# Four-layer graph network on one core: the one-hots of the matrix items read from a padded index row in three pieces

## The chip, the cores and the metric

The kernel runs on one core of one Trainium2 chip. The metric is the device time of one execution in microseconds (us), lower is better, given as the median of several executions. Engines are named as in the profile: PE (TensorE, matrix products), DVE (VectorE), ACT (ScalarE), POOL (GpSimd, which here issues the gathers), SP (SyncE, which here issues most plain transfers). DMA means a transfer between the chip's main memory and the on-chip memory.

## The reference

The input is `x` (6250 nodes x 128 features, float32) and a list of 100,000 edges `src`, `dst`. Four layers follow, each on `relu(layernorm(x))`, each added to `x`:

```
L0: h = f @ Wn.T;  new_h = [h[src], |h[dst]-h[src]|] @ We.T;  s = (h + segment_sum(new_h)) / count;  [f, s] @ Wl.T
L1: two graph transformer layers: scores q[dst].k[src] over 8 heads, clip, exp, segment sums, projection, FFN with GELU
L2: relu(D^-1/2 segment_sum((D^-1/2 f)[src] -> dst) @ W + b)
L3: two GCN convolutions and sigmoid(z @ Wd + bd)
```

Layers L2 and L3 need only sums over edges with weights that the nodes fix. The kernel therefore makes the adjacency matrix once (how many edges go from node i to node j) and does these layers as dense products. For layers L0 and L1 each edge's rows must be gathered.

## The kernel before

Nodes lie in 49 tiles of 128 (`NT`). The edges are sorted and cut into 832 steps of 128 edges (`STEPS`). Three **edge passes**, `diff` (layer L0), `att0` and `att1` (layer L1), go over all 832 steps in 208 groups of four steps (`S4`), four groups to a loop turn; between them lie dense stages, and after them the adjacency products ("the convolutions").

In an edge pass each engine has an order written out by hand (`body`), held together by semaphores. For a group:

- POOL gathers four blocks of 128 rows with four indirect DMAs (L720). The buffers hold several groups, so POOL runs ahead until it waits for a group to be used up (L1795 in the attention passes, the edge sums on PE in `diff`).
- DVE builds the edge one-hot (L1724), subtracts or multiplies gathered and expanded rows (L1771 in `diff`, L1780 in `att`), reduces to scores (L1783), clips (L1786), makes the messages (L1795) and adds PE's edge sums into `ACC` (L1737, L1739, L1742: `sums`).
- PE transposes one-hots (L886), expands rows (L896), sums edges (L914, L916, L918).
- ACT copies transposed one-hots (L1229) and takes `abs` (L1261) or `exp` (L1258).

**Matrix items** build the adjacency matrix beside this. An item is a set of up to 128 edges that share a source tile and a 512-wide group of destinations. For each item DVE writes two 16-bit one-hots by comparing an index row with a number for each edge: `OHS1` (128 wide, L1749) and `OHD` (512 wide, L1750). PE multiplies them (L926) into a bank of 128 x 512 sums, ACT keeps or clears the bank (L1242) and copies it out (L1247), SP stores it. There are 1456 items: 520 in `diff`, 520 in `att0` (in both, 3, 2, 3, 2 for the four groups of a turn) and 416 in `att1` (two for each group). The one-hots go round a ring of five (four in `att1`).

On DVE, the items of the next group are made at these places. In `diff`: after all four `sums` of the body, ahead of the next L1771. In the attention passes: the first item after `sums(1)` and ahead of L1795, which waits for ACT's `exp`; the second (and third) after `sums(2, 3)`, ahead of the next L1780. A body begins by loading four tile numbers into registers (L445).

`IOTA512` is the index row: the numbers 0 to 511 in float16, written once at L1603. L1749 reads its first 128 numbers.

Of the kernel before, what the change touches and what calls it, by code (L numbers as in the profile page):

```python
# [13 lines left out]
F16 = mybir.dt.float16  # L14
U16 = mybir.dt.uint16
I32 = mybir.dt.int32
ALU = mybir.AluOpType
# [3 lines left out]
P = 128  # L21
# [23 lines left out]
LOW = 10  # L45
T4 = 4
W4 = T4 * P
NW = -(-NT // T4)
ITEMS = STEPS + NT * (NW - 1)
CLASSES = NT * NW  # L50
PLAN = {"diff": (0, (3, 2, 3, 2), 5), "att0": (10 * STEPS // PB, (3, 2, 3, 2), 5), "att1": (20 * STEPS // PB, (2, 2, 2, 2), 4)}
SLOTS = 28 * STEPS // PB
SPARE = NW * P * NT
QJ = 7
# [3 lines left out]
NSC = STEPS // SCH  # L58
assert SLOTS >= ITEMS and STEPS // PB == GROUPS // 4 and NQ * QJ == NT and NSC * SCH == STEPS and NW == 13 and W4 == 512
AW = 2 * D + 1  # L60
# [15 lines left out]
def wait(eng, s, what, value, slot=None):  # L76

    if isinstance(value, int) and value <= 0:
        return
    eng.wait_ge(s[what] if slot is None else s[what][slot], value + s.base[what])  # L80
# [25 lines left out]
def build(nc, a, out, debug=None):  # L106
    with ExitStack() as ctx:
        def sb(name, shape, dt=F32):
            return ctx.enter_context(nc.sbuf_tensor(name, shape, dt))

        def sem(name):
            return ctx.enter_context(nc.semaphore(name))
# [5 lines left out]
        placed = [nc.dram_tensor(f"placed{o}", (2 * P * STEPS, 1), I32, kind="Internal").ap() for o in range(2)]  # L118
        adj_all = nc.dram_tensor("adj", ((NW + 2) * P, NT * W4), F32, kind="Internal").ap()
        adj = adj_all.rearrange("(g p) (j w) -> g p j w", p=P, w=W4)  # L120
        adj_blocks = adj_all.rearrange("r (j w) -> (r j) w", w=W4)

# [7 lines left out]
        TILE = [sb(f"TILE{o}", [P, STEPS], I32) for o in range(2)]  # L130
        IDX = [sb(f"IDX{o}", [P, STEPS], I32) for o in range(2)]
        SCR = sb("SCR", [P, 7296])
        ITEM = sb("ITEM", [P, 2 * W4 + 5 * (W4 + P) // 2])
        IOTA512 = sb("IOTA512", [P, W4], F16)
        IOTA = sb("IOTA", [P, P])
        IDENT = sb("IDENT", [P, P])
        ONES = sb("ONES", [P, P])
# [56 lines left out]
        LOK, DREL, KEEP = (Xf[:, i * SLOTS:(i + 1) * SLOTS] for i in range(3))  # L194
        at = 3 * SLOTS
        assert at + 3 * W4 <= NT * D
        STG = [Xf[:, at + i * W4:at + (i + 1) * W4] for i in range(3)] + [ITEM[:, i * W4:(i + 1) * W4] for i in range(2)]
        KEPT = STG[2]
        XS = [Xf[:, at:at + TG * D].rearrange("p (t d) -> p t d", t=TG), ITEM[:, 0:TG * D].rearrange("p (t d) -> p t d", t=TG)]
        assert TG * D <= 2 * W4  # L200
        OHD = ITEM[:, 2 * W4:2 * W4 + 5 * W4 // 2].bitcast(F16).rearrange("p (r w) -> p r w", r=5)
        OHS1 = ITEM[:, 2 * W4 + 5 * W4 // 2:].bitcast(F16).rearrange("p (r w) -> p r w", r=5)
        STORE = {"diff": TILE[0][32:33, :], "att0": TILE[1][32:33, :], "att1": TILE[0][64:65, :]}
        XA = Q
        IOTAK, REACHED = ACC[:, 0:ITEMS], ACC[:, ITEMS:2 * ITEMS]
# [49 lines left out]
        CLASS_SUM = [banks[1], banks[7]]  # L255
# [81 lines left out]
        def kind_of(n):  # L337
            return "att" if n.startswith("att") else "diff"
# [62 lines left out]
        for n, events in CONVS.items():  # L401
            cv[n] = Events(conv_sems)
            cv[n].base = dict(base)
            for k in events.split():
                base[k] += NW
        tiles_in, tiles_used = [sem(f"tiles_loaded{i}") for i in range(3)], sem("tiles_used")
# [20 lines left out]
        def sums_at(kind, j):  # L427

            if kind == "diff":
                return (j * 512, j * 512 + D) if j < 3 else (AW, 1024 + AW)  # L430
            return j * 256, None
# [308 lines left out]
        def _(pe):  # L740
# [84 lines left out]
            for k in range(2):  # L825
                ins = nc.tensor.matmul(R[0][:, k * 512:k * 512 + half], ONES[0:1, :], CEND[0:1, k * half:(k + 1) * half],
                                       start=True, stop=True)
# [7 lines left out]
            for c in range(NSC):  # L835
                ins = nc.tensor.matmul(R[0][0:SCH, c:c + 1], KEND[:, c * SCH:(c + 1) * SCH], IDENT[:, P - 1:P],
                                       start=True, stop=True)
# [37 lines left out]
            def edge_pass(name, o):  # L875
                s, kind = ps[name], kind_of(name)
                w = {"att": L1W, "diff": D}[kind]
                G = Gn
                restarts = PASSES.index(name)

                def transpose(it, u):
                    gi = it * 4 + u
                    wait(pe, s, "oh", gi + 1)
                    wait(pe, s, "oht", gi)
                    for j in range(S4):
                        ins = nc.tensor.transpose(R[0][:, j * P:(j + 1) * P], OH[:, u % 4, j, :], IDENT[:, :])  # L886
                    ins.then_inc(s["tr"], 1)

                def expand(it, u):

                    gi = it * 4 + u
                    tiles = step_tiles(pe, o, gi)
                    wait(pe, s, "oht", gi + 1)
                    wait(pe, s, "att", gi - 1)
                    for j in range(S4):
                        ins = nc.tensor.matmul(R[1][:, (u % 2) * 512 + j * P:(u % 2) * 512 + (j + 1) * P],  # L896
                                               OHT[:, u % 2, j, :], Qf[:, bass.ds(tiles[j] * D, D)],
                                               start=True, stop=True)
                    ins.then_inc(s["exp"], 1)

                def summed(it, u):
                    gi = it * 4 + u
                    wait(pe, s, "oh", gi + 1)
                    wait(pe, s, "msg", gi + 1)
                    if kind != "att":
                        wait(pe, s, "gath", (it + 1) * (16 * S4), u)

                    wait(pe, s, "acc", gi * S4)
                    for j in range(S4):
                        oh = OH[:, u % 4, j, :]  # L910
                        at, more = sums_at(kind, j)
                        dst = SUMS[:, at:at + w]
                        if kind == "att":
                            ins = nc.tensor.matmul(dst, oh, M[:, u % 2, j, :], start=True, stop=True)  # L914
                        else:
                            ins = nc.tensor.matmul(dst, oh, G[:, u, j, 0:w], start=True, stop=True)  # L916
                        if kind == "diff":
                            ins = nc.tensor.matmul(SUMS[:, more:more + D + 1], oh, M[:, u % 2, j, 0:D + 1],  # L918
                                                   start=True, stop=True)
                    ins.then_inc(s["agg"], 1)  # L920

                def item(i, k, ring):

                    pe.wait_ge(ad["built"], i + 1)
                    pe.wait_ge(ad["kept"], i + 1 + restarts)
                    nc.tensor.matmul(CLASS_SUM[k % 2], OHS1[:, k % ring, :], OHD[:, k % ring, :], start=False, stop=True,  # L926
                                     skip_group_check=True).then_inc(ad["summed"], 1)

                def body(it, u):
                    gi = it * 4 + u  # L930
                    own = items_of(name, it, u)
                    if exists(gi + 2):
                        transpose(it if u < 2 else it + 1, (u + 2) % 4)
                    item(*own[0])
                    if exists(gi + 1):
                        expand(it if u < 3 else it + 1, (u + 1) % 4)
                    item(*own[1])
                    summed(it, u)
                    for each in own[2:]:
                        item(*each)  # L940

                for bank in CLASS_SUM:
                    ins = nc.tensor.matmul(bank, ONES[:, :], ZERO[:, :].unsqueeze(1).broadcast_to([P, W4 // D, D]),
                                           start=True, stop=True)
                ins.then_inc(ad["opened"], 1)
                transpose(0, 0)
                transpose(0, 1)
                expand(0, 0)
                per_group(pe, body)
                end_phase(pe, "pe")  # L950
# [467 lines left out]
        def _(dve):  # L1418
            V = nc.vector
# [180 lines left out]
            V.tensor_tensor(KEND[:, 0:STEPS], KEND[:, 0:STEPS], IOTAK[:, 0:STEPS], ALU.add).then_inc(ad["ends"], 1)  # L1600
            V.memset(ONES16C, 1.0)
            c.link(V.tensor_tensor(JCOL, JCOL, STARTS0[:, :], ALU.add))
            V.tensor_copy(IOTA512[:, :], IOTAK[:, 0:W4])  # L1603
            c.link(V.tensor_copy(IOTAK16[:, 0:ITEMS], IOTAK))
            V.tensor_scalar(MARKS[0][:, 0:ITEMS], IOTAK16[:, 0:ITEMS], JCOL, None, ALU.is_ge).then_inc(ad["reach"], 1)
            dve.wait_ge(ad["endt"], 1)
# [110 lines left out]
            def edge_pass(name, o):  # L1717
                s, kind = ps[name], kind_of(name)
                w = {"att": L1W, "diff": AW}[kind]
# [24 lines left out]
                def item(i, k, ring):  # L1744

                    first = PLAN[name][0] + ring
                    if not isinstance(i, int) or i >= first:
                        dve.wait_ge(ad["summed"], i - (ring - 1))
                    V.tensor_scalar(OHS1[:, k % ring, :], IOTA512[:, 0:P], LOK[:, bass.ds(i, 1)], None, ALU.is_equal)  # L1749
                    V.tensor_scalar(OHD[:, k % ring, :], IOTA512[:, :], DREL[:, bass.ds(i, 1)], None, ALU.is_equal)\  # L1750
                        .then_inc(ad["built"], 1)

                def body(it, u):
# [320 lines left out]
```

## Time and profile before

| | |
|---|---|
| median of 3 runs | 7108.67 us (7102.15 to 7110.5) |
| the profiled execution, own time | 7118.68 us |
| its span | 7116.9 us |
| edge passes in the trace | about 1167 to 2303, 2637 to 3890 and 4257 to 5400 us |
| convolutions | from about 5610 us to the end |
| busy share of the span | PE 77%, DVE 62%, POOL 44%, ACT 41% |

The span is measured inside the execution and is 1.8 us shorter than the execution's own time; a microsecond gained or lost in the span is one in the time. Busy time of DVE counts overlapping instructions once.

### The profile page before, as it was taken

The numbers are of one execution on the slowest core, as the hardware profiler recorded it, in microseconds if no ns is written. First come the engines' busy times: TensorE is split into PE (matmuls) and PEld (weight loads), VectorE is DVE, ScalarE is ACT, GpSimd is POOL, SyncE is SP. The second block draws the span as 40 slices with busy tenths as digits, with TensorE's granted clock in tenths as the row PEclk, the third lists the DMA queues.
The fourth block names the chain that finished last, engine by engine and source line by source line (L and its number), as shares of the span: only waits on it lengthen the run. The fifth ranks groups of instructions, "written<-read, shape, count | busy, mean of one in ns | idle before, by whom it ended". The sixth has DMA issues, their size and how long they took to land. (4 is left out here: it accounts for less than half of the span.)

```text
span 7116.9 us, 123314 instructions
## 1 busy us (share of the span) xinstructions
PE 5456.4 (77%) x28313; PEld 3639.5 (51%) x28314; DVE 4436.3 (62%) x13076; ACT 2920.9 (41%) x5625; POOL 3117.5 (44%) x3096
## 2 busy tenths in 40 slices
PE   7987986777777556666666756666666899999998
PEld 3443444666665544554554545555554444444433
DVE  9999987777776567877777478888885311100000
ACT  2543543777776225555555425555553200000000
POOL 3754753777775016666665017777771000000000
PEclk9999997999999779889887878888887899999999
DMA  1000002555556116666667016666663477777799
GB/s 23 0 3 1 0 21 86 174 171 172 172 172 149 37 64 200 199 199 197 199 196 169 4 56 199 193 192 195 193 193 63 154 288 288 271 288 289 290 423 385
DMA packets 464533, 1168.30 MB, mean 164 GB/s; under 512 B 112062, under 2 KB 175102, under 8 KB 432156
## 3 DMA queue, kind: packets, MB, share of 16 engines
q1 hardware_dynamic: 337228, 892.75, 33.8%
q0 software_dynamic: 124928, 273.12, 16.1%
q10 hardware_dynamic: 2256, 0.89, 0.1%
q8 instruction: 67, 1.10, 0.1%
q14 instruction: 54, 0.44, 0.0%
HBM read 759.86 MB, written 405.30 MB: 164 GB/s over the span
## 5 line engine op out<-in xcount | busy, mean ns | idle before, releaser
L720 POOL DMA_INDIRECT ACC<-tab_kv,STAGE x1664 | 1661.5, 999 | 1430.3 <-DMA STAGE<-IDX 730.6
L1242 ACT ACTIVATE PS<-PS,X 128x512 f32<-128x512 f32 x1456 | 968.5, 665 | 525.2 <-PE PS L926 503.9
L914 PE MATMUL PS<-SCR 128*128 128x137 f32 x3328 | 596.7, 330 | 707.5 <-DVE ACC L1742 691.2
L720 POOL DMA_INDIRECT SCR<-tab_h,STAGE x832 | 827.6, 995 | 346.5 <-issue 274.4
L914 PEld LDWEIGHTS PS<-SCR 128*128 128x128 f32 x3328 | 496.3, 220 | 852.6 <-DVE ACC L1742 798.7
L1742 DVE TENSOR_TENSOR ACC<-ACC,PS 128x137 f32 (+1 forms) x2288 | 747.8, 327 | 247.7 <-PE PS L918 131.6
L1083 PE MATMUL PS<-ACC,Q 128*128 128x512 f32 (+3 forms) x2548 | 844.3, 577 | 49.5 <-DMA ACC<-adj 40.0
L787 PE MATMUL PS<-Q 128*128 128x416 f16 x4160 | 756.8, 340 | 60.9 <-DVE Q L1536 60.9
L896 PEld LDWEIGHTS PS<-Q,SCR 128*128 128x128 f32 x4992 | 712.5, 212 | 171.8 <-issue 146.8
L896 PE MATMUL PS<-Q,SCR 128*128 x4992 | 752.9, 299 | 59.2 <-issue 51.6
L681 POOL DMA_INDIRECT placed<-ACC,X x576 | 606.4, 1053 | 408.2 <-DVE X L1513 219.6
L926 PE MATMUL PS<-ITEM 128*128 128x512 f16 x1456 | 610.5, 419 | 154.8 <-ACT PS L1242 152.6
L1229 ACT ACTIVATE SCR<-PS 128x512 f32<-128x512 f32 x624 | 372.8, 597 | 814.5 <-PE PS L886 809.7
L787 PEld LDWEIGHTS PS<-Q 128*128 128x128 f16 x4160 | 390.4, 98 | 427.2 <-issue 141.9
L1083 PEld LDWEIGHTS PS<-ACC,Q 128*128 128x128 f32 (+1 forms) x2548 | 329.4, 165 | 505.0 <-issue 415.9
L1247 ACT ACTIVATE X<-PS 128x512 f32<-128x512 f32 x936 | 558.5, 597 | 45.0 <-DMA adj<-X 45.0
L1750 DVE TENSOR_SCALAR ITEM<-IOTA,X 128x512 f16<-128x512 f16 x1456 | 540.6, 371 | 0.0
L1083 PE MATMUL PS<-ACC,Y 128*128 128x512 f32 (+1 forms) x1274 | 524.4, 569 | 1.9 <-DMA ACC<-adj 1.5
L1534 DVE TENSOR_SCALAR Q<-Y,ACC 128x832 f16<-128x832 f16 x1040 | 448.0, 431 | 68.6 <-PE PS L787 68.6
L886 PE MATMUL PS<-IDENT,SCR 128*128 128x128 f32 x2496 | 445.5, 309 | 2.5 <-ACT SCR L1229 2.5
L916 PE MATMUL PS<-SCR 128*128 128x128 f32 x1664 | 341.4, 287 | 134.9 <-ACT SCR L1261 88.7
L1536 DVE TENSOR_SCALAR Q<-SCR,ACC 128x128 f16<-128x128 f16 x1560 | 435.3, 310 | 0.0
(297 smaller groups left out, 7481.6 us busy)
## 6 DMA issues: line engine op xcount, KB each, us to landing
ACC<-adj SPq DMA_DIRECT2D x252, 1792.0 KB, 6.8
adj<-X SPq DMA_DIRECT2D x936, 256.0 KB
adj<-ITEM SPq DMA_DIRECT2D x520, 256.0 KB
ACC<-tab_kv,STAGE POOLq DMA_INDIRECT x1664
SCR<-tab_h,STAGE POOLq DMA_INDIRECT x832
tab_kv<-SCR SPq DMA_DIRECT2D x14, 896.0 KB, 4.1
ACC<-adj SPq DMA_DIRECT2D x21, 448.0 KB, 4.1
placed<-ACC,X POOLq DMA_INDIRECT x576, 2.2
```

The costliest lines, as they stand in the source:

```text
L681: nc.gpsimd.indirect_dma_start(placed[o], bass.IndirectOffsetOnAxis(PLACE[:, c:c + 1], 0), CODE[:, c:c + 1], None).then_inc(s["scattered"] ...
L720: nc.gpsimd.indirect_dma_start(G[:, q, j, 0:w], None, table, bass.IndirectOffsetOnAxis(STAGE[:, u, q * S4 + j:q * S4 + j + 1], 0))\
L787: ins = nc.tensor.matmul(SUMS[:, at:at + w], OHP[:, u, k, :], OHS[:, u, q * w:(q + 1) * w], start=first and u == 0, stop=last and u == RIN ...
L896: ins = nc.tensor.matmul(R[1][:, (u % 2) * 512 + j * P:(u % 2) * 512 + (j + 1) * P], OHT[:, u % 2, j, :], Qf[:, bass.ds(tiles[j] * D, D)], ...
L914: ins = nc.tensor.matmul(dst, oh, M[:, u % 2, j, :], start=True, stop=True)
L926: nc.tensor.matmul(CLASS_SUM[k % 2], OHS1[:, k % ring, :], OHD[:, k % ring, :], start=False, stop=True, skip_group_check=True).then_inc(ad ...
L1083: ins = nc.tensor.matmul(banks[g % 2][half:half + w, 0:width(g)], rows[:, t, :], TILES3[m % 3][:, j, 0:width(g)], start=t < halves, stop=t ...
L1242: nc.scalar.activation(CLASS_SUM[(k + 1) % 2], CLASS_SUM[k % 2], ACT.Copy, scale=KEEP[:, bass.ds(i, 1)])\
L1247: nc.scalar.activation(STG[k % ring], CLASS_SUM[k % 2], ACT.Copy).then_inc(ad["out"], 1)
L1534: V.tensor_scalar(OHS[:, u, :], IOTAS16[:, 0:STEPS], SPR[:, at], None, ALU.is_equal)
L1742: V.tensor_tensor(dst, dst, SUMS[:, at:at + w], ALU.add).then_inc(s["acc"], 1)
L1750: V.tensor_scalar(OHD[:, k % ring, :], IOTA512[:, :], DREL[:, bass.ds(i, 1)], None, ALU.is_equal)\
```

## The change

The index row becomes two rows, one for each one-hot, each laid out as three pieces with a gap of two elements behind each piece: `IOTAW` is 3 x 172 numbers (0 to 515) at a pitch of 174, `IOTAN` is 3 x 44 numbers (0 to 131) at a pitch of 46. The one-hots are written as one run of 516 and 132 elements. Four elements more are made in each, which PE does not read: it takes the first 512 and the first 128.

```diff
+WIDE, NARROW = 3 * 172, 3 * 44
...
-        ITEM = sb("ITEM", [P, 2 * W4 + 5 * (W4 + P) // 2])
-        IOTA512 = sb("IOTA512", [P, W4], F16)
+        ITEM = sb("ITEM", [P, 2 * W4 + 5 * (WIDE + NARROW) // 2])
+        IOTAW = sb("IOTAW", [P, 3, WIDE // 3 + 2], F16)
+        IOTAN = sb("IOTAN", [P, 3, NARROW // 3 + 2], F16)
...
-                    nc.tensor.matmul(CLASS_SUM[k % 2], OHS1[:, k % ring, :], OHD[:, k % ring, :], start=False, stop=True,
+                    nc.tensor.matmul(CLASS_SUM[k % 2], OHS1[:, k % ring, 0:P], OHD[:, k % ring, 0:W4], start=False, stop=True,
...
-            V.tensor_copy(IOTA512[:, :], IOTAK[:, 0:W4])
+            V.tensor_copy(IOTAW[:, :, 0:WIDE // 3], IOTAK[:, 0:WIDE].rearrange("p (a b) -> p a b", a=3))
+            V.tensor_copy(IOTAN[:, :, 0:NARROW // 3], IOTAK[:, 0:NARROW].rearrange("p (a b) -> p a b", a=3))
...
-                    V.tensor_scalar(OHS1[:, k % ring, :], IOTA512[:, 0:P], LOK[:, bass.ds(i, 1)], None, ALU.is_equal)
-                    V.tensor_scalar(OHD[:, k % ring, :], IOTA512[:, :], DREL[:, bass.ds(i, 1)], None, ALU.is_equal)\
+                    V.tensor_scalar(OHS1[:, k % ring, :].rearrange("p (a b) -> p a b", a=3), IOTAN[:, :, 0:NARROW // 3], LOK[:, bass.ds(i, 1)], None, ALU.is_equal)
+                    V.tensor_scalar(OHD[:, k % ring, :].rearrange("p (a b) -> p a b", a=3), IOTAW[:, :, 0:WIDE // 3], DREL[:, bass.ds(i, 1)], None, ALU.is_equal)\
                         .then_inc(ad["built"], 1)
```

## Rows read from the trace of the kernel before

**Rows 1.** Busy time by stretch (diff, att0, att1): us, then each engine's, clock, DMA

```profile
1167.00:2303.00 1136.00, 879.03 (x6313) 726.12 (x6313) 850.86 (x2479) 781.72 (x1448) 827.63 (x832) 0.99 0.55 167
2637.00:3890.00 1253.00, 833.39 (x4646) 633.96 (x4646) 977.98 (x2882) 721.41 (x1438) 827.17 (x832) 0.87 0.65 194
4285.00:5400.00 1115.00, 758.11 (x4435) 640.21 (x4436) 913.55 (x2622) 597.26 (x1210) 804.95 (x804) 0.87 0.64 190
```

**Rows 2.** The same view, POOL's gathers (L720) alone, busy and count by stretch

```profile
1226.00:1396.00 170.00, 129.97 (x132) 1.00 0.54 174
1566.00:1736.00 170.00, 125.42 (x127) 1.00 0.54 171
...
4290.00:4480.00 190.00, 145.48 (x147) 0.88 0.65 200
```

**Rows 3.** The same stretches, DVE's edge one-hot (L1724) alone, one for each group

```profile
1226.00:1396.00 170.00, 21.21 (x31) 1.00 0.54 174
1566.00:1736.00 170.00, 21.92 (x32) 1.00 0.54 171
...
4290.00:4480.00 190.00, 24.02 (x35) 0.88 0.65 200
```

**Rows 4.** DVE's waits in diff: us in total, times, longest

```profile
DVE ACC L1742 <- PE PS L918: 126.3, 153, 3.2
DVE SCR L1771 <- issue: 58.4, 75, 1.4
```

**Rows 5.** DVE's waits in att0

```profile
DVE SCR L1795 <- ACT SCR L1258: 132.6, 106, 6.2
DVE SCR L1780 <- issue: 79.6, 150, 1.2
```

**Rows 6.** DVE's waits in att1

```profile
DVE SCR L1780 <- issue: 84.9, 194, 1.0
DVE SCR L1795 <- ACT SCR L1258: 63.2, 70, 6.4
```

**Rows 7.** The index row's readers over the run: ns min/median/max, first, last start

```profile
L1749 DVE TENSOR_SCALAR ITEM<-IOTA,X x1456: 233/248/500, 1166.7 to 5394.0; 128x128 f16<-128x128 f16 x182
L1750 DVE TENSOR_SCALAR ITEM<-IOTA,X x1456: 336/347/580, 1166.9 to 5394.2; 128x512 f16<-128x512 f16 x182
```

**Rows 8.** L1750 by pass (diff, att0, att1), groups view: busy us, mean ns

```profile
L1750 DVE TENSOR_SCALAR ITEM<-IOTA,X 128x512 f16<-128x512 f16 x470 | 187.6, 399 | 0.0
...
L1750 DVE TENSOR_SCALAR ITEM<-IOTA,X 128x512 f16<-128x512 f16 x482 | 172.8, 359 | 0.0
...
L1750 DVE TENSOR_SCALAR ITEM<-IOTA,X 128x512 f16<-128x512 f16 x342 | 120.4, 352 | 0.0
```

**Rows 9.** Other one-source DVE operations, groups view by form

```profile
L1453 DVE TENSOR_SCALAR Y<-Y 128x832 f16<-128x832 f16 x98 | 35.2, 372 | 2.5 <-PE PS L749 2.2
...
L1840 DVE TENSOR_SCALAR Y<-SCR 128x896 f32<-128x896 f32 x7 | 4.4, 628 | 0.2
...
L1423 DVE TENSOR_SCALAR ACC<-PS 128x832 f32<-128x832 f32 x3 | 3.1, 1024 | 6.4 <-PE PS L787 6.2 <-PE PS L749 0.2
...
L1866 DVE TENSOR_SCALAR BL<-BL 128x128 f32<-128x128 f32 x2 | 0.5, 226 | 0.1
```

**Rows 10.** POOL's gathers over the run: ns min/median/max, first and last start

```profile
L720 POOL DMA_INDIRECT ACC<-tab_kv,STAGE x1664: 940/946/1637, 2639.6 to 5371.7; - x185
```

**Rows 11.** Timeline in att1, DVE then ACT: start us, us, engine, line

```profile
4807.11 0.35 DVE L1750 TENSOR_SCALAR ITEM<-IOTA,X 128x512 f16<-128x512 f16 x1
4807.45 0.69 DVE L1795 TENSOR_TENSOR SCR<-ACC,SCR 128x512 f32<-128x512 f32 x1
...
4807.17 0.24 ACT L1258 ACTIVATE SCR<-SCR 128x32 f32<-128x32 f32 x1
```

**Rows 12.** The page, costliest groups: POOL's gathers, busy us and mean ns

```profile
L720 POOL DMA_INDIRECT ACC<-tab_kv,STAGE x1664 | 1661.5, 999 | 1430.3 <-DMA STAGE<-IDX 730.6
...
L720 POOL DMA_INDIRECT SCR<-tab_h,STAGE x832 | 827.6, 995 | 346.5 <-issue 274.4
```

More of the change, by code:

```diff
@@ L200, in build @@
         assert TG * D <= 2 * W4
-        OHD = ITEM[:, 2 * W4:2 * W4 + 5 * W4 // 2].bitcast(F16).rearrange("p (r w) -> p r w", r=5)
-        OHS1 = ITEM[:, 2 * W4 + 5 * W4 // 2:].bitcast(F16).rearrange("p (r w) -> p r w", r=5)
+        OHD = ITEM[:, 2 * W4:2 * W4 + 5 * WIDE // 2].bitcast(F16).rearrange("p (r w) -> p r w", r=5)
+        OHS1 = ITEM[:, 2 * W4 + 5 * WIDE // 2:].bitcast(F16).rearrange("p (r w) -> p r w", r=5)
         STORE = {"diff": TILE[0][32:33, :], "att0": TILE[1][32:33, :], "att1": TILE[0][64:65, :]}
```

## The prediction

> **What bounds the kernel now.** I read the busy time by stretch first [rows 1]. The changed instructions run only in the three edge passes, so these 3504 us of 7117 are all that can move. In none of them is an engine full: in `diff` PE is busy 879 of 1136 us and DVE 851, in `att0` DVE 978 of 1253, in `att1` DVE 914 of 1115. So a loop of waits through several engines, or POOL's issue rate, sets the pace.
>
> Next, who is ahead of whom. In a stretch near the beginning of `diff` POOL issues 132 gathers, 33 groups, in 170 us, 5.15 us a group, while the consumers make 31 groups; later both make 32 [rows 2, 3]. A group takes 1136 / 208 = 5.5 us over the pass, so POOL is close. In the beginning of `att1` it issues 147 gathers, 36.8 groups, while the consumers make 35. POOL runs ahead until its buffers are full and is then held to the consumers' pace, which is no better while POOL is free. I take from this that the consumers' loop (DVE, ACT, PE) is the bound in all three passes, by some 5% over POOL in `diff` and `att1`, and by more in `att0`.
>
> Last, DVE's waits, to see where in its order time can be added without harm. In `diff` it waits 126 us (153 of 208 groups) for PE's edge sums, behind L1771, and 58 us (75 groups) ahead of L1771 for its own sequencer [rows 4]. In `att0` L1795 waits for ACT's `exp` in 106 of 208 groups, 1.25 us each, and L1780 for the sequencer in 150 [rows 5]. In `att1` it is 70 groups of 208, 0.9 us each, and 194 [rows 6]. In `att1` DVE is the nearest thing to a bound: two thirds of its L1795 go off without an idle moment.
>
> **The change part by part.** *The instructions.* The 128-wide one-hot has a median of 248 ns, the 512-wide of 347 [rows 7]: (347 - 248) / 384 = 0.258 ns an element. Three one-source rows show what lies next to that. Contiguous float32 in SBUF goes at (628 - 226) / 768 = 0.523 ns, 832 elements from two PSUM rows take 1024 ns (over 1 ns an element), and 832 contiguous float16 elements 372 ns [rows 9]. So the rate has two factors of two: one that comes with 16-bit operands, one that is lost when layout or place doesn't suit. The change alters the layout and leaves 172 (44) adjacent 16-bit elements, so I take the loss of one factor, 0.523 ns. No row shows this form; the bounds are 0.258 ns (nothing lost) and 1.04 ns (both lost: 1024 less the 159 ns that the float32 line leaves at no element, over 832). Then L1750 goes to 347 + 516 x 0.523 - 512 x 0.258 = 485 ns (+138) and L1749 to 248 + 132 x 0.523 - 128 x 0.258 = 284 ns (+36): **+0.174 us an item**, and 1456 x 0.174 = 253 us of DVE time if no wait hid any.
>
> The Trainium skill ("VectorE: DVE Perf Modes", What auto-detection actually checks) says that the two-port modes need outermost counts of source and destination both even or equal. Read with a source of three rows and a destination of one run, it leaves two elements a cycle, by the page's 0.96 GHz an estimated 0.52 ns and the same sum; read with a destination of three rows, it leaves the op as fast as now, and the sum below would be nothing.
>
> *What lies on the path.* In the attention passes the first item stands ahead of L1795. Where L1795 waits for `exp` anyway, 1.25 or 0.9 us of wait hide 0.174. In `att0` 102 groups don't wait: 102 x 0.174 = **17.7 us**. In `att1` 138 don't, but many of these just meet: one `exp` ends at 4807.41, within L1750's run to 4807.46, and L1795 starts at 4807.45 [rows 11]. I take 0.10 for 0.174: **13.8 us** (nothing to 24.0).
>
> The items behind `sums(2, 3)` stand ahead of L1780. The register load that this waits for runs in the sequencer beside the one-hots, so the idle time can take them up: mean waits are 0.53 and 0.44 us. Groups without such a wait are 58 in `att0` and 14 in `att1` (three of them on a gather I leave aside, 11 remain): 58 x 0.174 = 10.1 and 11 x 0.174 = 1.9, **12.0 us**.
>
> In `diff` all two or three items stand ahead of L1771, and behind it DVE waits for PE in 153 groups, 0.83 us each, which hides 3 x 0.174 = 0.52. The other 55 groups could pay up to 0.52 each (29 us). But there the first L1750 often takes 0.57 us by a collision (below) that goes away, and part meets the sequencer's wait; I take a quarter, **7 us** (nothing to 29).
>
> PE's product and ACT's copies come behind the one-hots, but no wait for L1750 shows: a group's items are built a group ahead. Ring and stores are as before.
>
> *What it may take away.* L1750 is over its median in each pass: means 399, 359 and 352 against 347, that is 27, 6 and 2 us over 520, 520 and 416 items [rows 7, 8]. POOL's gathers, too: mean 999 and 995 against 946 [rows 10, 12], (0.053 x 1664) + (0.049 x 832) = 129 us. Both fit a resource that L1750 and the gather's issue hold in turn. At the lower rate it may be free. The 27 us in `diff` lie where DVE waits for PE and are counted above; of the 8 in the attention passes, with some more in L1749, half lies on the path: **-8 us**. The 129 us of POOL count nothing as long as the consumers are the bound; their cover is POOL's lead, and it grows as the consumers slow down.
>
> *The rest.* One cast in the preparation becomes two, an estimated microsecond at most, and a few hundred bytes more a partition cost no time.
>
> Sum: 17.7 + 13.8 + 12.0 + 7 - 8 = +42.5 us. The profiled execution would go from 7118.7 to 7161; the median, 10 us lower, from 7108.7 to **7151 us**, 0.6% slower.
>
> **The rivals.** *POOL freed, faster.* If POOL's issue were what spaces the groups, its 129 us would come back in `diff` and `att1` at least: 0.049 x 832 + 0.053 x 832 = 85 us, less the 28 us of `att0` above (17.7 + 10.1): 7108.7 - 85 + 28 = 7052. For it: 5.15 us is near 5.5, and the collisions are there. Against it: the stretches in which POOL is ahead and nothing goes faster [rows 2, 3]. It decides only if the consumers' own pace is below POOL's 5.15 us. A weaker form is that the DVE side of the collisions is on the path whole (27 + 6 + 2 = 35 us) and the longer items are hidden: 7074. Together 14%. The Trainium skill ("SBUF — State Buffer", Who interferes with whom) speaks for it: a DVE op in a two-port mode and GpSimd lock each other out of a shared pair of ports, and descriptors for POOL's DMAs need it. The trace agrees that both sides stretch, but not that this bounds.
>
> *Nothing to measure.* Either the engine keeps its rate, and the instructions take 348 and 249 ns (8%: three rows are an odd shape, but the elements within them still touch), or it halves it and the waits swallow all but some 10 us (12%): 7109 to 7119. For the second: 133 + 80 + 85 + 63 = 361 us of waits on DVE in the attention passes. Against: these come in some groups, the load comes in each.
>
> *One element a cycle.* Both factors lost: L1750 347 + 516 x 1.04 - 132 = 752 ns, L1749 352, +0.51 us an item, 742 us in all. The waits of [rows 4 to 6], 545 us, could hide at most that; I take 390, as some come where no item stands: +350 us, 7460. 5%.
>
> **How the numbers follow.** The forecast case, slower by 15 to 110 us, has 61%. Faster 14%, nothing 20%, one element a cycle 5%. 0.2% is 14 us, about what a measurement of this kernel can tell from no change. Slower is 61 + 5 = 66%, same 20%, faster 14%. The bounds of the forecast's terms give 17.7 + 0 + 0 + 0 - 8 = +10 at the low end; at the high end, with no item behind `sums(2, 3)` hidden in `att0` either (312 x 0.174 = 54), 17.7 + 24 + 54 + 29 = +125. For 8 in 10 the range leaves out most of the freed POOL and of the one-element case: 7090 to 7225.
>
> **What would show it.** In the changed trace: L1750 at 485 ns and L1749 at 284 in the median, none stretched to 0.57, gathers' mean near 950; DVE busy up by about 200 us over the passes; fewer waits of L1795 for ACT; passes longer by about 7 (`diff`), 25 (`att0`) and 12 us (`att1`); the other stages as they are; POOL waiting more than before for L1795. Wrong would be: `diff` and `att1` at POOL's pace of 5.15 us a group or less (rival one), 348 ns (rival two), 752 (rival three), or a longer stretch where the items hid, say by a loop through ACT that a later `exp` sets off.

## The result and the profile after

The changed kernel takes **7153.23 us** (median of 4 runs, 7151.29 to 7156.77); the kernel before, 7109.59 us (4 runs, 7102.15 to 7117.46). The ratio is **1.0066, interval 1.0054 to 1.0078**: slower by 38 to 55 us. Forecast were 7151 us and slower. Of the 28 timings of the kernel before that the first four experiments are set against, one took 8777 us and is left out of their ratios; the other 27 lie between 7102 and 7129 us.

The line's view of the index row's readers and of POOL's gathers in the changed kernel, over the whole run (ns min/median/max, first and last start), answers to [rows 7] and [rows 10]:

```profile
L1752 DVE TENSOR_SCALAR ITEM<-IOTAN,X x1456: 267/275/285, 1166.8 to 5428.2; 128x132 f16<-128x132 f16 x182
L1753 DVE TENSOR_SCALAR ITEM<-IOTAW,X x1456: 465/473/479, 1167.0 to 5428.4; 128x516 f16<-128x516 f16 x182
...
L722 POOL DMA_INDIRECT ACC<-tab_kv,STAGE x1664: 940/946/1480, 2633.5 to 5407.3; - x185
L722 POOL DMA_INDIRECT SCR<-tab_h,STAGE x832: 938/944/1442, 1169.5 to 2277.8; - x167
```

The wide one-hot went from 347 to 473 ns in the median and the narrow one from 248 to 275. What is at least as telling is the third figure: the longest of 1456 is 479 ns, where it was 580. No one-hot is stretched any more. POOL's gathers still reach 1480 ns. The page's costliest groups (busy us, mean ns) answer to [rows 12]:

```profile
L722 POOL DMA_INDIRECT ACC<-tab_kv,STAGE x1664 | 1641.8, 987 | 1487.7 <-DMA STAGE<-IDX 724.1
...
L722 POOL DMA_INDIRECT SCR<-tab_h,STAGE x832 | 813.2, 977 | 358.8 <-issue 261.4
```

So POOL was relieved of 19.7 + 14.4 = 34 us and not of 129: the means fell from 999 to 987 and from 995 to 977, not to 946. And the relief turned into waiting: its idle time before the attention gathers rose from 1430 to 1488 us.

DVE's waits in `diff`, `att0` and `att1` (us in total, times, longest) answer to [rows 4 to 6]:

```profile
DVE ACC L1745 <- PE PS L920: 124.8, 202, 4.1
DVE SCR L1774 <- issue: 29.5, 56, 1.2
...
DVE SCR L1798 <- ACT SCR L1260: 125.6, 110, 10.2
DVE SCR L1783 <- issue: 46.5, 93, 0.8
...
DVE SCR L1783 <- issue: 53.3, 108, 0.9
DVE SCR L1798 <- ACT SCR L1260: 53.3, 69, 6.9
```

Two lines of the kernel before belong beside them. The stretch of [rows 5] stops at 3890 us, 16 us before the pass ends on DVE, and leaves out its last long waits; over the whole pass (2633 to 3910 us; the changed kernel's is read to 3925) the wait for `exp` was 143 us and not 133. And in `diff` DVE also waited for its own sums:

```profile
DVE SCR L1795 <- ACT SCR L1258: 143.0, 109, 7.5
...
DVE ACC L1742 <- DVE ACC L1742: 13.2, 50, 0.5
```

And busy time by stretch (us, busy time of PE, weight load, DVE, ACT, POOL, then clock, DMA share and GB/s), which answers to [rows 1]; the second and third stretch are longer or later, as the passes are:

```profile
1167.00:2303.00 1136.00, 880.86 (x6330) 727.57 (x6331) 903.58 (x2489) 784.88 (x1452) 813.18 (x832) 0.99 0.55 168
2637.00:3910.00 1273.00, 834.77 (x4631) 634.49 (x4629) 1043.98 (x2872) 722.13 (x1438) 806.49 (x830) 0.87 0.64 191
4300.00:5440.00 1140.00, 764.96 (x4460) 645.73 (x4458) 974.12 (x2638) 600.75 (x1216) 805.26 (x805) 0.87 0.63 187
```

DVE's busy time rose by 53, 66 and 61 us, 179 in all. A pass can be measured from the start of its first gather to that of its last; the changed kernel's row for `att0` runs from 2633.5 to 3894.3 us (below, beside the experiments'), before it was 2639.6 to 3874.3. Each figure is that of one profiled execution:

| first to last gather | `diff` | `att0` | `att1` |
|---|---|---|---|
| before | 1110.5 | 1234.7 | 1124.6 |
| after | 1108.3 (-2.2) | 1260.8 (+26.1) | 1142.7 (+18.1) |

By DVE's own work, from the start of the first L1780 to the end of the last L1795, the two attention passes are 22.3 us longer (1251.5 to 1273.8) and 17.2 us (1143.1 to 1160.3). The two executions differ by 34.6 us in their spans: +42 in the three passes and -7.5 in the rest, most of it in the stretches between the passes.

In `diff` everything fits into waits that were there: L1774 waits 29 us less for the sequencer and 5 us less for a gather, and the 13 us for DVE's own sums are gone; the wait for PE's edge sums is what it was (126 and 125 us). In `att0` the items take 71 us more busy time (wide, mean 358 to 472 ns; narrow, 254 to 276; 0.136 us by 520), 17 + 33 = 50 us of it comes out of the two waits, and 21 is left for a pass that is 22 longer on DVE. In `att1` it is 416 x 0.136 = 57 us, 10 + 32 = 42 out of the waits, 15 left, 17 measured.

### The profile page after: what moved, and what is told of

It reads as the page before. It is cut to its first block and busy times, and to the rows that moved or that the text cites. A ratio compares the mean times of both kernels' runs of the same rounds, so it can differ in the third digit from the quotient of the medians.

```text
span 7151.5 us, 123315 instructions
## 1 busy us (share of the span) xinstructions
PE 5462.7 (76%) x28313; PEld 3644.3 (51%) x28314; DVE 4613.4 (65%) x13077; ACT 2923.2 (41%) x5625; POOL 3083.5 (43%) x3096
## 5 line engine op out<-in xcount | busy, mean ns | idle before, releaser
L722 POOL DMA_INDIRECT ACC<-tab_kv,STAGE x1664 | 1641.8, 987 | 1487.7 <-DMA STAGE<-IDX 724.1
L722 POOL DMA_INDIRECT SCR<-tab_h,STAGE x832 | 813.2, 977 | 358.8 <-issue 261.4
L1745 DVE TENSOR_TENSOR ACC<-ACC,PS 128x137 f32 (+1 forms) x2288 | 748.9, 327 | 234.9 <-PE PS L920 124.8
L1753 DVE TENSOR_SCALAR ITEM<-IOTAW,X 128x516 f16<-128x516 f16 x1456 | 687.8, 472 | 0.0
```

Source lines behind the costliest of these rows:

```text
L722: nc.gpsimd.indirect_dma_start(G[:, q, j, 0:w], None, table, bass.IndirectOffsetOnAxis(STAGE[:, u, q * S4 + j:q * S4 + j + 1], 0))\
L1745: V.tensor_tensor(dst, dst, SUMS[:, at:at + w], ALU.add).then_inc(s["acc"], 1)
L1753: V.tensor_scalar(OHD[:, k % ring, :].rearrange("p (a b) -> p a b", a=3), IOTAW[:, :, 0:WIDE // 3], DREL[:, bass.ds(i, 1)], None, ALU.is_e ...
```

## The experiments

The first four were run on a chip on which the kernel before took 7113.01 us (28 runs). The other eight ran on three other chips, on which the kernel before itself took 8795, 8726 and 8721 us, so only lengths of instructions and ratios against its runs there are read from them.

### Is it the gaps or the three? Four pieces

The same gaps of two, but four pieces of 128 and of 32 elements.

```diff
-WIDE, NARROW = 3 * 172, 3 * 44
+PIECES = 4
+WIDE, NARROW = W4, P
...
-        IOTAW = sb("IOTAW", [P, 3, WIDE // 3 + 2], F16)
-        IOTAN = sb("IOTAN", [P, 3, NARROW // 3 + 2], F16)
+        IOTAW = sb("IOTAW", [P, PIECES, WIDE // PIECES + 2], F16)
+        IOTAN = sb("IOTAN", [P, PIECES, NARROW // PIECES + 2], F16)
```

> Only the shape of the reading differs from the changed kernel: four pieces of 128 (and of 32) with the same gaps of two, 512 and 128 elements written. If the halved rate comes from three source rows against one destination run, an even count of rows gives the old rate back: the 512-wide one-hot at 347 ns and the 128-wide at 248 ns in the median, stretched ones of 570 ns in the first edge pass again, and the time of the kernel before, 7109 us within 14. If the gaps themselves cost, the two stay at 473 and 275 ns and the time is near 7150 us.

7117.62 us (10 runs), ratio 1.0005 [0.9996, 1.0015]. Its readers and gathers:

```profile
L1753 DVE TENSOR_SCALAR ITEM<-IOTAN,X x1456: 233/248/499, 1167.9 to 5398.0; 128x128 f16<-128x128 f16 x182
L1754 DVE TENSOR_SCALAR ITEM<-IOTAW,X x1456: 336/347/580, 1168.1 to 5398.1; 128x512 f16<-128x512 f16 x182
...
L723 POOL DMA_INDIRECT ACC<-tab_kv,STAGE x1664 | 1664.0, 1000 | 1429.1 <-DMA STAGE<-IDX 720.6
L723 POOL DMA_INDIRECT SCR<-tab_h,STAGE x832 | 828.2, 995 | 345.6 <-issue 275.8
```

Every figure is that of before, the collisions with it (580 ns, gathers 1000 and 995). The gaps cost the instructions nothing, and the kernel nothing that the interval (-3 to +11 us) can tell. It is the three pieces read against one run written that halve the rate and free the gathers of these collisions.

### Which items pay? Ahead or behind

In the attention passes, only the items behind `sums(2, 3)` read the three pieces and the one ahead of L1795 the old row ("fast ahead"), or the other way round ("slow ahead"). A contiguous `IOTA512` is kept beside for it. The items of `diff` read the pieces in the first and the old row in the second. To make room, `IOTAN` shares its place with a row of ones and is written later, ahead of the passes.

```diff
-                def item(i, k, ring):
+                def item(i, k, ring, pieces=True):
...
-                            item(*each)
+                            item(*each, pieces=False)
...
-                            item(*each)
+                            item(*each, pieces=True)
```

> In the attention passes the item ahead of the messages (L1798 of the changed kernel) is built the old way, those behind sums(2, 3) and all of the first pass the new way. My theory, that the price is paid almost only where DVE doesn't wait for exp: the third pass gets nearly all back, the second about 15 of its 24 us, the first pass stays as in the changed kernel (-3): 7117 us. The rival, that each slow item costs the same wherever it stands: 312 of 520 items of the second pass and 208 of 416 of the third stay slow, so 24 x 0.6 + 17 x 0.5 - 3 = +20, 7129 us.

> The complement: only the item ahead of the messages in the attention passes is built the new way, all others the old way. My theory: the second pass pays 15, the third 15 to 17 us, the first nothing: 7140 us. The rival, the same price everywhere: 24 x 0.4 + 17 x 0.5 = +18, 7127 us.

Fast ahead: 7118.89 us (10 runs), 1.0005 [0.9996, 1.0015]. Slow ahead: 7142.91 us (5 runs), 1.0036 [1.0023, 1.0049]. The `att0` gathers of fast ahead, of slow ahead and of the whole change:

```profile
L723 POOL DMA_INDIRECT ACC<-tab_kv,STAGE x832: 940/946/1469, 2636.0 to 3873.8; - x167
```

```profile
L723 POOL DMA_INDIRECT ACC<-tab_kv,STAGE x832: 940/947/1482, 2639.1 to 3886.1; - x167
```

```profile
L722 POOL DMA_INDIRECT ACC<-tab_kv,STAGE x832: 940/946/1453, 2633.5 to 3894.3; - x167
```

`att0` is 3.1 us longer with fast ahead, 12.3 with slow ahead, and 26.1 with both; `att1` 3.2, 16.1 and 18.1. Of `att0` the old one-hots give nearly one length (1234.7 before, 1236.3 with four pieces, 1236.8 in the next experiment), of `att1` they don't (1124.6, 1134.1, 1134.2), so `att1`'s three differences carry 10 us of doubt. The recorded 7117 and 7140 us lie within both intervals, 7110 to 7124 and 7129 to 7148 us, the rivals' 7129 and 7127 outside. The waits in `att0` tell why, first of fast ahead, then of slow ahead (there L1805 is the messages, L1790 the product ahead of the scores):

```profile
DVE SCR L1805 <- ACT SCR L1261: 141.9, 109, 7.7
DVE SCR L1790 <- issue: 48.7, 97, 0.8
```

```profile
DVE SCR L1805 <- ACT SCR L1261: 123.0, 110, 6.4
DVE SCR L1790 <- issue: 77.0, 148, 1.1
```

Between these two traces an item behind differs by 0.128 us in the mean (wide 366 and 472 ns, narrow 255 and 277) and an item ahead by 0.154 (345 and 471, 246 and 274). Slower items behind eat the wait for the sequencer (79.6 before, 48.7 now, 31 of the 40 us that 312 x 0.128 makes) and leave the other wait (143.0 and 141.9). Slower items ahead eat some of the wait for `exp` (143.0 to 123.0, 20 of the 32 us that 208 x 0.154 makes) and leave the first. That is the split of the prediction: the item ahead of L1795 pays most. But the parts don't add up to the whole in `att0`: 3.1 + 12.3 = 15.4 against 26.1. In `att1` they do, 19.3 against 18.1, within its doubt. By the ratios it is 4 + 26 = 30 us against 47, each with 7 to 9 us of uncertainty. In `att0` one or the other alone may still use slack that both together have used up; that reading is argued, not shown by a run of its own.

### Does `diff` gain by itself?

The pieces in `diff` alone, `pieces=kind == "diff"`, the old row in both attention passes.

```diff
-                def item(i, k, ring):
+                def item(i, k, ring, pieces=kind == "diff"):
```

> The new one-hots in the first edge pass alone, the old ones in both attention passes. In the changed kernel that pass was 3 us shorter though DVE had 53 us more to do. My theory (DVE waits for PE's edge sums there in most groups, so the items hide): 7106 us, 0 to 6 us faster than before, which may not be measurable. The rival that the load counts wherever it stands: 520 of 1456 items by 44 us, +16, 7125 us.

7119.13 us (11 runs), 1.0003 [0.9994, 1.0012]. Its gathers, attention and `diff`:

```profile
L723 POOL DMA_INDIRECT ACC<-tab_kv,STAGE x1664 | 1660.6, 998 | 1435.8 <-DMA STAGE<-IDX 723.4
L723 POOL DMA_INDIRECT SCR<-tab_h,STAGE x832 | 812.2, 976 | 361.4 <-issue 261.9
```

Where the pieces are read, the gathers' mean falls to 976 ns, where not, it stays at 998. The `diff` pass took 1110.0 us against 1110.5. So 520 one-hot pairs that are 0.09 us longer in the mean cost nothing in `diff`, and 15 us of POOL given back there gain nothing. By the ratio the kernel is at 7109 to 7122 us. The rival's 7125 lies outside, and so does 7106; of the first theory's "0 to 6 us faster" the end near zero fits.

### What are the rates? Three rows on both sides, and a step of two

The first reads three pieces and writes three pieces with gaps into `OHD` and `OHS1`; the matrix product then takes the gaps too, so that the adjacency matrix is another one.

```diff
-                    V.tensor_scalar(OHD[:, k % ring, :].rearrange("p (a b) -> p a b", a=3), IOTAW[:, :, 0:WIDE // 3], DREL[:, bass.ds(i, 1)], None, ALU.is_equal)\
+                    V.tensor_scalar(OHD[:, k % ring, :].rearrange("p (a b) -> p a b", a=3)[:, :, 0:WIDE // 3], IOTAW[:, :, 0:WIDE // 3], DREL[:, bass.ds(i, 1)], None, ALU.is_equal)\
```

> The changed kernel, but the one-hots are written in three rows too, with the same gaps of two as the index rows; PE still takes the first 512 and 128 elements, gaps among them, so the adjacency matrix in it is not the reference's, while every instruction and transfer is as before. If the rate depends on source and destination having unequal outer counts (three against one), three against three gives the old rate: 347 and 248 ns, stretched instructions again, time within 14 us of before. If an odd count or the gaps alone halve it, 473 and 275 ns and about 7153 us.

Ratio 1.003 [1.0017, 1.0043] (7 runs, 8821.63 against 8795.03 us). Its readers:

```profile
L1753 DVE TENSOR_SCALAR ITEM<-IOTAN,X x1456: 241/258/431, 1896.6 to 7057.6; 128x132 f16<-128x132 f16 x182
L1754 DVE TENSOR_SCALAR ITEM<-IOTAW,X x1456: 372/421/615, 1896.7 to 7057.8; 128x516 f16<-128x516 f16 x182
```

Neither 347 nor 473 but 421 ns, and stretched ones up to 615 again. So with three rows on both sides the one-hots do collide with the gathers. Why it is 421 no run tells. Nor was the time "within 14 us": 0.3% more is 15 to 38 us there.

The second is the kernel before with the index numbers two elements apart, in one row.

```diff
-        IOTA512 = sb("IOTA512", [P, W4], F16)
+        IOTA512 = sb("IOTA512", [P, W4, 2], F16)
...
-                    V.tensor_scalar(OHD[:, k % ring, :], IOTA512[:, :], DREL[:, bass.ds(i, 1)], None, ALU.is_equal)\
+                    V.tensor_scalar(OHD[:, k % ring, :], IOTA512[:, :, 0], DREL[:, bass.ds(i, 1)], None, ALU.is_equal)\
```

> The kernel before, with the index row's elements two apart, so that no pair is adjacent. If the 16-bit factor hangs on adjacent elements and the other one does not outlive it, about 750 ns and 350 ns, the bound that the prediction named; two elements a cycle, as for float32, would be 480 and 280 ns. With +0.5 us an item my theory (waits hide it only until they are used up) gives more than in proportion: the change paid 44 us for 0.153 us an item, proportion gives 145 us, 7255; with all waits used up 742 less 390 us, 7450.

> The kernel of e6, with the index row's elements two apart, timed again. Its one-hots took 491 and 280 ns in the median there, as long as in the changed kernel (473 and 275), but some took up to 690 ns, so they still collide with the gathers as before the change. The two kernels therefore differ in the collisions alone. My theory, POOL's lead hides what collisions cost POOL, and DVE's side of them is worth some 10 to 20 us: 7165 to 7175 us. The rival, the collisions' 129 us of POOL were worth much and hid a larger cost of the change: above 7210 us.

> The kernel of e6 and e9 once more: as slow one-hots as the changed kernel has, but with collisions. If the kernel before takes near 7110 us here: my theory, POOL's lead hides what the collisions cost POOL and DVE's side of them is worth 10 to 20 us, 7165 to 7175 us; the rival, collisions worth much, above 7210 us. If the kernel before takes 8700 us or more again, no difference, as in e6 and e9.

Three times: 1.0007 [0.9997, 1.0017], 0.9986 [0.997, 1.0002], 1.0006 [0.9993, 1.002], ten runs each. The readers in the first:

```profile
L1749 DVE TENSOR_SCALAR ITEM<-IOTA,X x1456: 267/280/478, 1897.4 to 7054.5; 128x128 f16<-128x128 f16 x182
L1750 DVE TENSOR_SCALAR ITEM<-IOTA,X x1456: 470/491/690, 1897.6 to 7054.7; 128x512 f16<-128x512 f16 x182
```

I had expected about 750 ns, both factors of two lost. It is 491, one factor: here the collisions stay (690 ns), in the change they go (479 ns). So there are two ways to halve the rate. I read it so: elements that don't touch lose what 16-bit numbers gain by touching and keep the resource that is shared with POOL; three pieces against one run keep the first and give up the second. With 144 ns more on L1750 the time did not move on these chips, where DVE has more idle time (busy 1109 of 1550 us in a stretch over `att0`, 978 of 1253 in [rows 1]). It says nothing about a chip that runs at 7.1 ms, so the 7165 to 7175 us of the expectation stay untested.

### Is POOL the bound? Fills in its queue

After each group's gathers POOL fills a small tile of its own: 16 elements once ("small"), or 256 elements twice ("large"). The kernel is otherwise the one before.

```diff
+        EXTRA = sb("EXTRA", [P, 256])
...
+                        for k in range(2):
...
+                            nc.gpsimd.memset(EXTRA[:, :], 0.0).then_inc(extra, 1)
```

> The kernel before with one small POOL fill (16 elements) behind the four gathers of each group, with its own semaphore: an estimated 0.15 us more of POOL a group. My theory, POOL ahead of the consumers by 0.2 to 0.3 us a group: no pass gets longer, 7113 within 14. The rival, POOL as the bound: 2 passes x 208 x 0.15 = 62 us more, 7171.

> The same with two fills of 256 elements for each group, an estimated 0.6 us more of POOL a group. My theory: first and third pass become bound by POOL and pay 208 x (0.6 - 0.25) = 73 us each, the second, where consumers are 0.8 us a group slower than POOL, pays nothing: 7255 us. The rival, POOL as the bound in all passes now: 3 x 208 x 0.6 = 374, 7480.

> The kernel of e8 timed again: two POOL fills of 256 elements for each group, 0.32 us each there, with waits 0.7 us more of POOL a group. My theory: first and third pass become bound by POOL and pay 208 x (0.7 - 0.25) = 94 us each, the second, where the consumers are 0.8 us a group slower than POOL, at most 10: 7300 us. The rival, POOL as the bound in all passes now: 3 x 208 x 0.7 = 437, 7550.

Small: 1.0005 [0.9992, 1.0018]. Large: **0.9605 [0.9589, 0.9621]** and, again, **0.956 [0.9539, 0.9581]**, 4% faster with more work, where every expectation was slower. The large fill, first and second time:

```profile
L731 POOL MEMSET EXTRA<- 128x256 f32 x1248 | 405.0, 324 | 96.3 <-issue 77.0 <-POOL EXTRA L731 19.0
```

```profile
L731 POOL MEMSET EXTRA<- 128x256 f32 x1248 | 411.2, 329 | 96.3 <-issue 73.2 <-POOL EXTRA L731 22.7
```

Two fills a group put 411 us of busy time on POOL and the passes became shorter: `att0` had 1318 us from first to last gather, against 1500 in the step of two, timed beside it on the same chip. The next lines are from the two kernels' `att0`, first the step of two, then the large fills:

```profile
POOL ACC L720 <- DVE SCR L1795: 381.4, 127, 6.2
ACT PS L1242 <- remote: 281.9, 87, 5.4
```

```profile
ACT PS L1250 <- remote: 69.6, 31, 4.1
ACT SCR L1237 <- remote: 17.6, 6, 4.3
```

"Remote" is a releaser that the profile can't name; the traces of before and after at 7.1 ms have not one such wait. Where POOL is slowed, those of ACT's L1242 shrink from 282 to 70 us. What they are is open: no run here tells a cause, and I don't read the 4% as anything about the change. For the question that the fills were to settle, POOL's lead at 7.1 ms, they are worth nothing.

### All items behind

The kernel before with the first item of the attention passes moved behind `sums(2, 3)` as well.

```diff
-                        for each in ahead[0:1]:
-                            item(*each)
...
-                        for each in ahead[1:]:
+                        for each in ahead:
```

> The kernel before with one thing moved: in the attention passes all items of the next group are built behind sums(2, 3), none ahead of the messages (L1795). e2 and e3 showed 0.153 us to cost 12 and 16 us a pass ahead of the messages and about 3 behind. My theory: the 0.43 us of DVE that an item takes are on the path ahead of the messages in 102 and 138 groups, and behind sums(2, 3) the wait for the sequencer takes up part of them: 10 to 60 us faster than before. The rival, that there they delay the next group's scores instead, so that nothing is won: within 14 us, or slower if L1795 then only waits longer for exp.

1.001 [0.9999, 1.0022] (12 runs, 8735.52 against 8720.95 us): the gain of 10 to 60 us did not come there, and for a chip at 7.1 ms it is inconclusive.

## Why the prediction was right, point by point

**The rate.** One factor of two was lost, as taken: +126 and +27 ns over the medians, **0.153 us an item where 0.174 was forecast**. The rate was right, 0.52 ns an element: (473 - 275) / (516 - 132) = 0.516. The constant was off: 473 - 516 x 0.516 = 207 ns at no element, where [rows 7] give 347 - 512 x 0.258 = 215, and 516 x (0.523 - 0.516) = 4 ns more. The Trainium skill ("VectorE: DVE Perf Modes", What auto-detection actually checks) has it that the two-port modes need outermost counts both even or equal. The four pieces (347 ns) and the three against one run (473) agree with it, and so do the stretched ones at three rows on both sides, which its "equal" lets in.

**`att0` and `att1`.** Forecast were 17.7 + 10.1, less some of the relief, "about 25"; measured 26.1 from gather to gather and 22.3 on DVE. And 13.8 + 1.9, "about 12"; measured 18.1, of which an uncertain part is the pass's own scatter: it took 1134 us, 9 more than before, also in the two kernels whose attention one-hots keep the old rate (four pieces, `diff` only). The two passes together are 44 us longer, against 37 forecast. The division is right as well: the item ahead of the messages costs most. The count of 102 groups of `att0` that don't wait for `exp` came from the stretch that ends too early; over the whole pass it was 99, and is 98 after. The working behind it may be too simple: it charges each item alone, and in `att0` slower items at both places cost more together than one by one. No run shows where that comes from.

**`diff`, the term that was mis-sized.** I took a quarter of 29 us, +7. It was -2.2 in the changed kernel and -0.5 with `diff` alone. The sequencer's wait took up 29 us (58.4 to 29.5), the wait for DVE's own sums 13, and the items are only 0.09 us longer in the mean there, since the 399 ns of [rows 8] were full of collisions that went away. The first and the last I had named and given too little. The wait for PE's edge sums, which was to hide most, hid nothing by its total: 126 us before and 125 after, in 202 groups in place of 153.

**The relief.** L1750's collisions went whole, in the direction of the -8; no run gives its size. "Gathers' mean near 950" was wrong: 987 and 977. I had put all of their stretch down to the matrix items. The traces can be sorted by what DVE was doing when a gather began, over all 2496 gathers. In the kernel before, 464 began under a matrix item and took 1001 ns in the mean, 25 us over 946 in all; 612 began under the edge one-hot (L1724) or the messages (L1795) and took 1116, 104 us. So the items were never the cause of more than a fifth of the 129 us. After, 729 began under an item and took 944 ns, none over 957, and 536 under L1727 or L1798 took 1126, 97 us (last section).

**POOL counts nothing.** This step held, as far as the runs reach: 34 us of POOL were given back and its idle time before the gathers grew by 57 and 12 us. `diff` alone, with 15 us given back, is 0.5 us shorter, where the rival in which POOL is the bound would have had all 15 back. In the attention passes the relief and the longer items can't be told apart, and a direct trial with POOL slowed at 7.1 ms is missing.

**The forecasts by themselves.** DVE's busy time was to grow by about 200 us and grew by 179; waits of L1795 for ACT were to be fewer, and are as many (109 and 110 in `att0`, 70 and 69 in `att1`) but 17 and 10 us less in all. "The other stages as they are" was off by 7.5 us in this pair of executions.

So the sum came out at 7151 against 7153 partly by errors that cancel: `diff` 9 us too high, the attention passes together some 7 too low, and the price of an item 14% too high against a loop that passes on more of it than single groups show. The last two microseconds are luck: against the profiled execution of before the sum gave 7161, and the changed kernel's profiled execution took 7153.2; the 10 us taken off for the median belong to an execution of before that happened to be slow.

## What to carry to other kernels

Before a layout in pieces goes into a hot vector instruction, look at its median with the pieces in the source and in the destination: here the gaps were free and three pieces against one run cost half the rate. Other odd counts were not tried. Price such a change by the waits that stand right behind the instruction, place by place: in `att0`, ahead of 80 us of waiting, 40 us of longer instructions cost 3; ahead of a wait that half of the groups don't have, 32 us cost 12. Then allow for more when both come together: there they cost 26. And taking a collision off an engine that is ahead bought waiting time only.

## What the runs showed of the hardware

**Gathers stretch under two-input vector work.** With the matrix items free of collisions, all that is left of stretched gathers in the changed kernel, 407 of 2496 over 1 us, began while the edge one-hot (L1727) or the messages (L1798) ran; both read two operands from on-chip SBUF. The 1960 that began under nothing or under any other DVE instruction, among them the two-input ones that read one operand from PSUM (L1745, L1774, L1783), took 960 ns at most. DVE and then POOL in one stretch of `att1` (start us, us), and again at another:

```profile
4902.99 0.68 DVE L1727 TENSOR_TENSOR SCR<-IOTA,LO 128x512 f32<-128x512 f32 x1
```

```profile
4903.18 1.31 POOL L722 DMA_INDIRECT ACC<-tab_kv,STAGE  x1 [0.30 <-issue]
4904.80 0.94 POOL L722 DMA_INDIRECT ACC<-tab_kv,STAGE  x1 [0.30 <-issue]
```

```profile
4914.60 0.68 DVE L1727 TENSOR_TENSOR SCR<-IOTA,LO 128x512 f32<-128x512 f32 x1
```

```profile
4914.63 1.47 POOL L722 DMA_INDIRECT ACC<-tab_kv,STAGE  x1 [0.30 <-issue]
```

The first gather begins 0.19 us into the edge one-hot and ends 4904.49 - 4903.67 = 0.82 us after it. The second begins 0.03 us into it and ends 4916.10 - 4915.28 = 0.82 us after. Both last as if they began near the end of that instruction; the gather at 4904.80 with nothing of the kind beside it takes 0.94. The Trainium skill ("SBUF — State Buffer", Who interferes with whom) infers that such a two-input operation does not hold up POOL's descriptors; these rows speak against that. No run took L1727 away, so it is read from the trace and not tried.

**Two ways to halve the rate.** 516 elements from three pieces to one run take 473 ns and never collide. 512 elements with a step of two take 491 ns and do (690). Three pieces on both sides take 421 ns and do (615).

**Chips at 8.7 to 8.8 ms.** The same kernel took some 23% longer, with waits for no named releaser, and became 4% faster with 1248 fills added to POOL. In the step of two, second time, the 1.6 ms more than before lie ahead of the passes (first gather at 1902 us against 1169) and in them (first to last gather 1422, 1500 and 1468 us against 1110, 1235 and 1125), and not behind them (1736 us from the last gather on, against 1745). Open.
